# Moving the epilogue's transposes to another accumulator and the next head's block-maximum pass eight iterations later, in an eight-core attention kernel

## The chip, the cores and the metric

The kernel runs on all eight cores of one Trainium2 chip, four cores on each of two dies. Every core gets two of the sixteen sequences and runs the same program on them; nothing is exchanged between cores. The metric is the device time of the slowest core in microseconds (us): the median of three runs before is 6212.64 us (6209.49 to 6223.26).

## What is computed

The output is `x + attention(xn) + ffn(xn)`, with `xn` the layer norm of `x`, shape 16 x 2048 x 1024. The attention has 16 heads of 64 columns and selects 32 x 32 blocks:

```
Qh, Kh, Vh = block means of Q, K, V over 32 rows
low  = Qh @ Kh.T / 8 ; row_max = low.max(-1)
norm = low - row_max + 5000 near the diagonal
hi_mask = norm >= (1024th largest value of norm)
hi   = Q_block @ K_block.T / 8 for the selected blocks      # exact scores
max_vals = running maximum of hi per query
num  = sum exp(hi - max_vals) @ V, corrected, + low part for the other blocks
den  = the same sums without V, corrected, + 1e-6
out  = num / den
```

The running maximum enters the result in the kernel only through the small constant of the denominator, so each head needs, beside the sums of exponentials, a maximum of its scores over every selected 32 x 32 block.

## The kernel before

Engines are TensorE (PE), VectorE (DVE), ScalarE (ACT), GpSimd (POOL) and SyncE (SP, it only issues DMAs). A recorder writes one instruction list for each engine; each list runs in order. Every instruction except those of PE first waits for the one before it on its own engine, and every DMA of an SP or POOL list waits for the landing of the DMA before it in that list. All ordering between engines is by counting semaphores.

The program first normalises `x`, transposes the weights, runs the feed-forward half and the threshold search; it writes `x + ffn` to the DRAM array `part_sc`. The attention stage follows, from about 2300 us to the end. It has eight passes, one for each pair of heads. A pass does

1. the projections of Q and K for both heads (`qtp`, `ktp`), 128 matmuls into the two halves of the PSUM tile `pA`,
2. the V projection and its transposes, between which the block-maximum pass (called phase A here) of the first unit runs,
3. four units: two heads by two sequences. Unit 0 is the first one of a pass, unit 3 the last.

A unit is 32 iterations `kg` (`emit_chunk_iter`, L824). Iteration `kg` issues on PE two score matmuls S(kg) into `pS[kg % 2]` (L835), then two matmuls AV(kg-1) (L801) that add the product of the exponentials with V into `pO`, then, if there is a next unit in the pass, two halves of phase A for that next unit (`emit_phaseA_half`, L746): one matmul of 512 columns into one half of `pA` (L758), and on DVE a maximum over each group of 32 columns (L766); every fourth half adds the mask `bx` and reduces once more (L773, L776). ACT does one exponential of 128 x 1024 an iteration (L848). There are 64 halves to a unit, so two an iteration in units 0 to 2, and none in unit 3. After iterations 15 and 31 ACT copies `pO` to `outT` (L820, called the evacuation here).

`emit_prep` (L699) is called for the next unit before the 32 iterations. On POOL's list it waits for the end of the last unit's matmuls and then issues four DMAs, one after another: `rhsc`, `lhsc`, `bx`, `rmb` (L705 to L713). Half 0 of phase A waits on PE for the landing of `bx`. On SP's list it loads the slice of `part_sc` for the next unit into `xtile` (L719). On DVE it writes the mask rows of `rhsc` (L724) and three small tiles; ACT turns these into `laT` (L740).

The epilogue (`emit_epilogue`, L853) follows the unit: 16 transposes of `outT` with 128 columns each into `pS[0]` and `pS[1]` (L860), two additions and one reciprocal on DVE (L869, L874), 16 activations of 128 x 64 that scale into `stage` (L881), an addition of `xtile` on POOL (L891) and the store (L895). Since `pS` is used, S(0) of the next unit waits for all 16 activations:

```
if kg == 0:
    r.wait("tensor", "sGP", state["ngp_prep"][par])
    r.wait("tensor", "sDV", state["ndv_prep"][par])
    r.wait("tensor", "sDV", state["ndv_ep"])
    r.wait("tensor", "sAC", state.get("nac_ep", 0))
```

The addition stands in POOL's list ahead of the next `emit_prep`.

Of the kernel before, what the change touches and what calls it, by code (L numbers as in the profile page):

```python
# [11 lines left out]
AF = mybir.ActivationFunctionType  # L12
ALU = mybir.AluOpType
# [82 lines left out]
def build_program(debug=False, trunc=None):  # L96
# [17 lines left out]
    part_sc = nc.dram_tensor("part_sc", [T, C], F32).ap()  # L114
# [18 lines left out]
    with stack:  # L133
        r = Rec(nc, stack)
# [6 lines left out]
        id_f = sb("id_f", [128, 128], F32)  # L141
# [16 lines left out]
        eps_all = sb("eps_all", [128, NBH * 16], F32)  # L158
# [47 lines left out]
        with contextlib.ExitStack() as st_p0:  # L206
# [135 lines left out]
            def bh_idx(p, hip, s):  # L342
                return (2 * p + hip) * 2 + s
# [304 lines left out]
        with contextlib.ExitStack() as st_p2:  # L648
# [33 lines left out]
            def bh_idx(p, hip, s):  # L682
# [14 lines left out]
                     "nst_a2": [0, 0]}  # L697

            def emit_prep(p, hip, sq, par, prev_chunk_pe):  # L699
                b = bh_idx(p, hip, sq)  # L700
# [45 lines left out]
            def emit_phaseA_half(p, hip, sq, u):  # L746
# [105 lines left out]

            def emit_epilogue(p, hip, sq, par):  # L853
                b = bh_idx(p, hip, sq)
                r.wait("tensor", "sAC", state["prev_evac"])
                r.wait("tensor", "sDV", state["ndv_ep"])
                slot_off = [0, 128, 256, 384, 512, 640, 768, 896]
                for i in range(16):
                    so = slot_off[i % 8]
                    r.emit("tensor", lambda e, i=i, so=so: e.transpose(  # L860
                        pS[i // 8][:, so:so + 65],
                        outT[:, i * 128:(i + 1) * 128], id_f[0:65, 0:65]))
                npe_tr = r.cnt["sPE"]
                stg = stage2[par]
                r.wait("vector", "sPE", npe_tr)
                r.wait("vector", "sSY", state["nst_a2"][par])
                r.wait("scalar", "sSY", state["nst_a2"][par])
                for h2 in range(2):
                    r.emit("vector", lambda e, b=b, h2=h2: e.tensor_tensor(  # L869
                        rdenw16[:, h2 * 8:(h2 + 1) * 8],  # L870
                        pS[h2].ap().rearrange("p (a c) -> p a c", a=8)[:, :, 64:65]
                        .rearrange("p a c -> p (a c)"),
                        eps_all[:, b * 16 + h2 * 8:b * 16 + (h2 + 1) * 8], ALU.add))
                ndv_rd = r.emit("vector", lambda e: e.reciprocal(  # L874
                    rdenw16[:, :], rdenw16[:, :]))
                r.wait("scalar", "sDV", ndv_rd)
                nac_ep = 0
                for i in range(16):
                    so = slot_off[i % 8]
                    nac_ep = r.emit("scalar", lambda e, i=i, so=so, stg=stg:  # L880
                                    e.activation(  # L881
                                        stg[:, i * 64:(i + 1) * 64],
                                        pS[i // 8][:, so:so + 64], AF.Identity,
                                        scale=rdenw16[:, i:i + 1]))
                state["ndv_ep"] = r.cnt["sDV"]
                state["nac_ep"] = nac_ep
                h = 2 * p + hip
# [12 lines left out]
            state["nls_next"] = 0  # L900
            for p in range(8):
# [11 lines left out]
                for tag, dst in [("q", qtp), ("k", ktp)]:  # L913
                    for n in range(8):
                        slot = n % 2
                        r.wait("tensor", "sAC", pcons[slot])
                        r.wait("tensor", "sDV", state["phA_dv2"][slot])
# [22 lines left out]
                for half in range(2):  # L940
                    vev = [0] * 4
                    for n4 in range(4):
                        n = half * 4 + n4
                        slot = n % 2
                        r.wait("tensor", "sAC", pcons[slot])
                        r.wait("tensor", "sDV", state["phA_dv2"][slot])
# [48 lines left out]
                for i in range(4):  # L995
# [8 lines left out]
                    emit_epilogue(*bhs[i], par)  # L1004
# [80 lines left out]
```

How the kernel before makes its waits and increments, by code:

```python
    def emit(self, eng, fn):  # L57
        sname = ESEM[eng]
        n = 16 if eng in ("sync", "gpsimd") else 1
        if eng != "tensor" and self.cnt[sname]:
            self.wait(eng, sname, self.cnt[sname])
        self.cnt[sname] += n
        h = self.sem[sname]
        self._push(eng, lambda e, fn=fn, h=h, n=n: fn(e).then_inc(h, n))
        return self.cnt[sname]
# [1 line left out]
    def wait(self, eng, sname, val):  # L67
        if not val:
            return
        h = self.sem[sname]
        self._push(eng, lambda e, h=h, v=val: e.wait_ge(h, v))
```

## Time and profile before

| what | value |
|---|---|
| median of the runs | 6212.64 us |
| the profiled execution's own time | 6235.19 us |
| span of its slowest core (core 1) | 6233.6 us |
| spans of all cores | 6191.9 to 6233.6 us |
| PE / DVE / ACT / POOL busy | 50% / 40% / 27% / 3% of the span |
| DVE L766, 2048 reductions | 1416.7 us busy |
| ACT L848, 1024 exponentials | 1048.6 us busy |
| PE L758, L835, L801, 2048 each | 872.5, 696.4, 678.5 us busy |

The profiled execution is one of many, and 22.6 us longer than the median. "Busy" is a share of the whole span, which has stages with different limits. PEclk is the clock that TensorE was granted, as a share of 2.4 GHz: 1.00 is 2.4 GHz and 0.50 is 1.2 GHz.

### The profile page before, as it was taken

How to read it: one execution, taken by the hardware profiler on the slowest of the kernel's cores; microseconds unless marked ns; L12 is line 12 of the kernel's file. 1: busy time of each engine (PE TensorE's matmuls, PEld its weight loads, DVE VectorE, ACT ScalarE, POOL GpSimd, SP SyncE). 2: the span in 40 equal slices, each digit the busy share in tenths (PEclk: the TensorE clock that was granted, in tenths of full speed). 3: DMA queues.
4: the chain of work that ended last, by engine and by line, in shares of the span. 5: the costliest groups of instructions: out<-in, count | busy, mean ns of one | idle time of the engine just before them, and what ended most of it. 6: DMA issues, size and time to landing. Idle time of an engine off the chain costs nothing.

```text
span 6233.6 us, 53657 instructions; the slowest of 8 cores (6191.9 to 6233.6 us)
## 1 busy us (share of the span) xinstructions
PE 3145.2 (50%) x11513; PEld 1101.5 (18%) x11513; DVE 2502.1 (40%) x5239; ACT 1708.6 (27%) x2627; POOL 212.2 (3%) x269
## 2 busy tenths in 40 slices
PE   1121113333333426666666666566566666657656
PEld 0021001111111111122222112122122112112112
DVE  3522133343344315533633552551561551642553
ACT  2200000000000002452442343344344334335235
POOL 0000100000000000000000000000000000000000
PEclk9955557667766856776886777787687678678678
DMA  1243002222212310001001001000100010010010
GB/s 61 63 81 68 2 15 68 67 59 64 68 41 59 83 46 23 18 14 29 14 17 23 21 17 23 21 14 17 29 14 17 16 28 16 18 28 14 14 24 11
DMA packets 457371, 206.62 MB, mean 33 GB/s; under 512 B 428746, under 2 KB 429938, under 8 KB 456882
## 3 DMA queue, kind: packets, MB, share of 16 engines
q1 hardware_dynamic: 420946, 138.85, 9.1%
q0 software_dynamic: 36128, 64.34, 4.4%
q8 instruction: 121, 1.98, 0.1%
q14 instruction: 176, 1.44, 0.1%
HBM read 150.62 MB, written 47.73 MB: 32 GB/s over the span
## 4 chain that ended last, share of the span: by engine, by line
PE 30%; DMA 23%; DVE 22%; ACT 12%; issue 11%; DVEq 1%; ACTq 0%; POOL 0%; POOLq 0%; SPq 0%
DVE bm L766 10%; PE pA L758 7%; PE pS L835 6%; ACT aT L848 6%; PE pO L801 5%; DMA bx<-bsm_dram 4%; PE pA L920 4%; DMA fW<-wT_r 3%; ACT stage L881 3%; PE pA L516 3%; DMA fW<-wT_v 2%; DMA fW<-wT_k 2%; DMA rhsc<-qtp 2%; DMA nb<-norm_all 2%; DVE fA L501 2%
## 5 line engine op out<-in xcount | busy, mean ns | idle before, releaser
L766 DVE TENSOR_REDUCE bm<-pA 128x16 f32<-128x512 f32 x2048 | 1416.7, 692 | 1340.0 <-PE pA L758 1152.5
L848 ACT ACTIVATE aT<-pS 128x1024 bf16<-128x1024 f32 x1024 | 1048.6, 1024 | 1176.8 <-PE pS L835 1144.8
L758 PE MATMUL pA<-ktp,qtp 64*128 64x512 bf16 x2048 | 872.5, 453 | 805.6 <-DMA bx<-bsm_dram 477.9
L835 PE MATMUL pS<-rhsc,lhsc 128*128 128x512 bf16 x2048 | 696.4, 426 | 216.9 <-ACT stage L881 186.4
L801 PE MATMUL pO<-aT,vtm 128*65 128x512 bf16 x2048 | 678.5, 416 | 196.1 <-ACT aT L848 187.3
L516 PE MATMUL pA<-fA,fW 128*128 128x512 bf16 x1536 | 414.6, 422 | 291.8 <-DMA fW<-wT_r 75.7
L758 PEld LDWEIGHTS pA<-ktp,qtp 64*128 64x128 bf16 x2048 | 186.6, 96 | 1478.4 <-issue 1469.4
L417 PE MATMUL pB<-bis_cnt,ones 128*128 128x32 f32 x116 | 35.1, 396 | 684.4 <-DVE bis_cnt L413 684.4
L801 PEld LDWEIGHTS pO<-aT,vtm 128*65 128x65 bf16 x2048 | 223.0, 120 | 538.0 <-issue 458.1
L869 DVE TENSOR_TENSOR rdenw<-pS,eps_all 128x8 f32<-128x8 f32 x64 | 10.7, 167 | 616.9 <-PE pS L860 612.5
L516 PEld LDWEIGHTS pA<-fA,fW 128*128 128x128 bf16 x1536 | 151.2, 105 | 549.4 <-issue 438.5
L835 PEld LDWEIGHTS pS<-rhsc,lhsc 128*128 128x128 bf16 x2048 | 142.0, 101 | 546.7 <-issue 501.8
L547 ACT ACTIVATE fR<-pA 128x512 bf16<-128x512 f32 x64 | 38.2, 597 | 717.1 <-PE pA L516 717.1
L920 PE MATMUL pA<-xnT,wsl_q 128*128 128x512 bf16 x512 | 135.1, 434 | 169.3 <-DMA out<-stage 104.5
L881 ACT ACTIVATE stage<-pS,rdenw 128x64 f32<-128x64 f32 x512 | 160.8, 314 | 150.5 <-DVE rdenw L874 106.0
L581 ACT ACTIVATE fA<-fB 128x512 bf16<-128x512 bf16 x64 | 40.3, 629 | 477.4 <-DVE fB L574 472.3
L986 ACT ACTIVATE vtm<-pS 128x64 bf16<-128x64 f32 x256 | 57.5, 224 | 392.4 <-PE pS L977 390.2
L547 ACT ACT_TABLE_LOAD x1 | 1.3, 1283 | 596.4 <-PE pA L516 596.4
L891 POOL TENSOR_TENSOR stage<-stage,xtile 128x1024 f32<-128x1024 f32 x32 | 74.7, 2336 | 2401.4 <-ACT stage L881 2401.4
L417 PEld LDWEIGHTS pB<-bis_cnt,ones 128*128 128x128 f32 x116 | 29.0, 311 | 694.0 <-issue 694.0
L949 PE MATMUL pA<-xnT,wsl_v 128*128 128x512 bf16 x512 | 137.5, 436 | 2.2 <-DVE bm L766 2.2
L773 DVE TENSOR_TENSOR bmm<-bm,bx 128x64 f32<-128x64 f32 x512 | 115.5, 226 | 53.2
(139 smaller groups left out, 2307.9 us busy)
## 6 DMA issues: line engine op xcount, KB each, us to landing
xtile<-x SPq DMA_DIRECT2D x64, 512.0 KB
fW<-wT_r SPq DMA_DIRECT2D x64, 256.0 KB
fW<-wT_k SPq DMA_DIRECT2D x64, 256.0 KB
fW<-wT_v SPq DMA_DIRECT2D x64, 256.0 KB
xtile<-part_sc SPq DMA_DIRECT2D x32, 512.0 KB
bx<-bsm_dram POOLq DMA_DIRECT2D x32, 512.0 KB, 8.0
out<-stage SPq DMA_DIRECT2D x32, 512.0 KB
part_sc<-ptile POOLq DMA_DIRECT2D x16, 512.0 KB, 3.0
```

Of the source, the lines that this page charges most:

```text
L501: e.scalar_tensor_tensor(d[:, c * QT:(c + 1) * QT], xnT[:, base:base + QT], mucol[m][:, c:c + 1], d[:, c * QT:(c + 1) * QT], ALU.mult, ALU ...
L516: e.matmul(pA[:, sl * 512:sl * 512 + QT], w[:, cc * 128:(cc + 1) * 128], rb[:, cc * QT:(cc + 1) * QT], start=(cc == 0), stop=(cc == 7)))
L758: e.matmul(pA[:, half * 512:(half + 1) * 512], qtp[p0:p0 + 64, ts0 + t * 128:ts0 + (t + 1) * 128], ktp[p0:p0 + 64, ts0 + kq * 512:ts0 + (k ...
L766: nred = r.emit("vector", lambda e, kq=kq, half=half: e.tensor_reduce(bm[:, kq * 16:(kq + 1) * 16], pA[:, half * 512:(half + 1) * 512] .re ...
L773: r.emit("vector", lambda e, b=b, t=t: e.tensor_tensor(bmm[:, :], bm[:, :], bx[:, t * 64:(t + 1) * 64], ALU.add))
L801: e.matmul(pO[:, sl * 512:(sl + 1) * 512], vtm[:, (sq * 16 + k) * 130 + hip * 65: (sq * 16 + k) * 130 + hip * 65 + 65], aT[bpar][:, sl * 5 ...
L835: e.matmul(pS[bpar][:, sl * 512:(sl + 1) * 512], lhs2[par][:, k * 128:(k + 1) * 128], rhs2[par][:, qh * 1024 + sl * 512: qh * 1024 + (sl + ...
L848: e.activation(aT[bpar][:, :], pS[bpar][:, :], AF.Exp, scale=0.125))
L881: e.activation(stg[:, i * 64:(i + 1) * 64], pS[i // 8][:, so:so + 64], AF.Identity, scale=rdenw16[:, i:i + 1]))
L891: "gpsimdc", lambda e, par=par, stg=stg: e.tensor_tensor(stg[:, :], stg[:, :], xtile[par][:, :], ALU.add))
L920: e.matmul(pA[:, slot * 512:(slot + 1) * 512], wsl[tag][:, cc * 128:(cc + 1) * 128], xnT[:, cc * T + n * 512:cc * T + (n + 1) * 512], star ...
L949: e.matmul(pA[:, slot * 512:(slot + 1) * 512], wsl["v"][:, cc * 128:(cc + 1) * 128], xnT[:, cc * T + n * 512: cc * T + (n + 1) * 512], sta ...
```

## The change

Three things are done.

- The epilogue of units 0 to 2 no longer uses `pS`. Its 16 transposes go in two waves of eight into `pA`. Wave 0 (eight transposes, one addition, one reciprocal, eight activations) stands at the end of the unit; wave 1 stands in iteration 4 of the next unit, after AV(3) on PE and ahead of exponential 4 on ACT, and with it the POOL addition and the store. S(0) waits for neither. The epilogue of unit 3 stays as it was.
- Phase A of the next unit, which `pA` is needed for, is spread over iterations 8 to 31: three halves in each of iterations 8 to 23, two in each of iterations 24 to 31. Iterations 0 to 7 have none.
- The load of the `part_sc` slice is issued again just ahead of its use (in `finish`), while the load in `emit_prep` stays: 32 loads of 512 KB more.

```diff
@@ emit_phaseA_half
+                if u < 2:
+                    r.wait("tensor", "sAC", state["pA_free_ac"][half])
+                    r.wait("tensor", "sDV", state["ndv_ep"])
@@ emit_chunk_iter
                 if kg == 0:
                     r.wait("tensor", "sGP", state["ngp_prep"][par])
                     r.wait("tensor", "sDV", state["ndv_prep"][par])
-                    r.wait("tensor", "sDV", state["ndv_ep"])
-                    r.wait("tensor", "sAC", state.get("nac_ep", 0))
@@
-                if nxt is not None:
-                    emit_phaseA_half(*nxt, 2 * kg)
-                    emit_phaseA_half(*nxt, 2 * kg + 1)
+                if kg == 4 and state["pending_w1"] is not None:
+                    state["pending_w1"]()
+                    state["pending_w1"] = None
+                if nxt is not None and kg >= 8:
+                    if kg < 24:
+                        us = range((kg - 8) * 3, (kg - 8) * 3 + 3)
+                    else:
+                        us = range(48 + (kg - 24) * 2, 48 + (kg - 24) * 2 + 2)
+                    for u in us:
+                        emit_phaseA_half(*nxt, u)
@@ emit_epilogue, units 0 to 2 (unit 3 keeps the old form)
+                    r.wait("tensor", "sDV", max(state["phA_dv2"][0],
+                                                state["phA_dv2"][1]))
+                    def emit_wave(w, gate0=0, gate1=0):
+                        if gate0:
+                            r.wait("tensor", "sAC", gate0)
+                        acts = []
+                        for sl8 in range(8):
+                            i = w * 8 + sl8
+                            if gate1 and sl8 == 4:
+                                r.wait("tensor", "sAC", gate1)
+                            r.emit("tensor", lambda e, i=i, sl8=sl8: e.transpose(
+                                pA[:, sl8 * 128:sl8 * 128 + 65],
+                                outT[:, i * 128:(i + 1) * 128], id_f[0:65, 0:65]))
...
+                        ndv_rd = r.emit("vector", lambda e, w=w: e.reciprocal(
+                            rdenw16[:, w * 8:(w + 1) * 8],
+                            rdenw16[:, w * 8:(w + 1) * 8]))
+                        r.wait("scalar", "sDV", ndv_rd)
...
+                        for sl8 in range(8):
+                            i = w * 8 + sl8
+                            acts.append(r.emit(
+                                "scalar", lambda e, i=i, sl8=sl8, stg=stg:
+                                e.activation(stg[:, i * 64:(i + 1) * 64],
+                                             pA[:, sl8 * 128:sl8 * 128 + 64],
+                                             AF.Identity,
+                                             scale=rdenw16[:, i:i + 1])))
+                        return ndv_rd, acts
+                    _, acts0 = emit_wave(0)
+                    def w1fn(acts0=acts0, b=b, par=par, stg=stg, h=h, sq=sq):
+                        ndv_rd, acts1 = emit_wave(1, gate0=acts0[3], gate1=acts0[7])
+                        state["ndv_ep"] = ndv_rd
+                        state["nac_ep"] = acts1[7]
+                        state["pA_free_ac"] = [acts1[3], acts1[7]]
+                        finish(b, par, stg, h, sq, acts1[7])
+                    state["pending_w1"] = w1fn
@@ new function, the end of every epilogue
+            def finish(b, par, stg, h, sq, nac_ep):
+                r.wait("sync", "sGC", state["ngp_add"][par])
+                nld = r.emit("sync", lambda e, h=h, sq=sq, par=par: e.dma_start(
+                    xtile[par].ap().rearrange("p (i d) -> p i d", i=16),
+                    part_sc.rearrange("(s i pp) c -> s pp i c", i=16, pp=128)
+                    [sq][:, :, h * 64:(h + 1) * 64]))
                 r.wait("gpsimdc", "sAC", nac_ep)
-                r.wait("gpsimdc", "sSY", state["nsy_part"][par])
+                r.wait("gpsimdc", "sSY", nld)
```

The projections' waits on `pA` take the later of their old value and the waves' last activations.

## Rows read from the trace of the kernel before

**Rows 1.** Who waited for whom, core 1: us in total, times, longest us.
```profile
PE pA L758 <- DMA bx<-bsm_dram: 477.9, 32, 18.8
...
PE pS L835 <- ACT stage L881: 186.4, 24, 8.0
```

**Rows 2.** Timeline between units 0 and 1 of the third pass: start, us, engine, instruction.
```profile
3516.50 1.02 ACT L820 ACTIVATE outT<-pO 65x1024 f32<-65x1024 f32 x1 [2.32 <-PE pO L810]
...
3517.77 1.97 PE L860 MATMUL pS<-id_f,outT 65*128 65x65 f32 x16 [1.42 <-ACT outT L820]
3519.98 0.44 DVE L869 TENSOR_TENSOR rdenw<-pS,eps_all 128x8 f32<-128x8 f32 x2 [7.38 <-PE pS L860]
...
3520.92 6.41 ACT L881 ACTIVATE stage<-pS,rdenw 128x64 f32<-128x64 f32 x16 [3.40 <-DVE rdenw L874]
...
3527.43 0.35 ACT L740 ACTIVATE laT<-la_t,cln 64x64 bf16<-64x64 f32 x1
...
3528.64 1.02 ACT L848 ACTIVATE aT<-pS 128x1024 bf16<-128x1024 f32 x1 [0.87 <-PE pS L835]
3529.90 0.57 POOL L705 DMA_DIRECT2D rhsc<-qtp  x1
...
3546.80 1.01 PE L758 MATMUL pA<-ktp,qtp 64*128 64x512 bf16 x2 [18.30 <-DMA bx<-bsm_dram]
```

**Rows 3.** Windows from evacuation to the first reduction L766, 16 units 1 and 2: columns below.
```profile
core 1: us, PE busy (x) PEld busy (x) DVE busy (x) ACT busy (x) POOL busy (x), PEclk, DMA share, GB/s
...
3516.50:3547.55 31.05, 3.73 (x20) 2.15 (x20) 2.40 (x7) 7.42 (x19) 4.55 (x5) 0.50 0.30 68
...
sum 488.09, PE 59.74 PEld 34.30 DVE 38.45 ACT 118.64 POOL 72.88; mean PE 3.73 PEld 2.14 DVE 2.40 ACT 7.42 POOL 4.55
```

**Rows 4.** Windows from first to last reduction L766, 16 units 1 and 2; then sum of 8 units 0.
```profile
3547.55:3613.06 65.51, 55.90 (x189) 16.39 (x188) 50.97 (x94) 31.74 (x31) 0.26 (x1) 0.91 0.01 1
...
sum 1059.55, PE 897.06 PEld 263.22 DVE 815.25 ACT 507.86 POOL 4.08; mean PE 56.07 PEld 16.45 DVE 50.95 ACT 31.74 POOL 0.25
...
sum 535.38, PE 462.23 PEld 133.73 DVE 407.67 ACT 253.93 POOL 2.49; mean PE 57.78 PEld 16.72 DVE 50.96 ACT 31.74 POOL 0.31
```

**Rows 5.** Timeline of ACT in unit 1, third pass: exponentials 4 iterations apart, 2.4 GHz.
```profile
3557.20 1.02 ACT L848 ACTIVATE aT<-pS 128x1024 bf16<-128x1024 f32 x1 [0.48 <-PE pS L835]
...
3564.86 1.02 ACT L848 ACTIVATE aT<-pS 128x1024 bf16<-128x1024 f32 x1 [0.56 <-PE pS L835]
```

**Rows 6.** The chain that ended last, one iteration of unit 0 at 1.2 GHz.
```profile
3447.51 0.97 PE pS L835 x2
...
3449.33 0.97 PE pA L758 x2
3450.30 0.97 PE pS L835 x2
```

**Rows 7.** Timeline of ACT in unit 3 of the third pass: pairs of exponentials, no phase A.
```profile
3738.70 2.14 ACT L848 ACTIVATE aT<-pS 128x1024 bf16<-128x1024 f32 x2 [0.20 <-PE pS L835]
3741.05 2.14 ACT L848 ACTIVATE aT<-pS 128x1024 bf16<-128x1024 f32 x2 [0.20 <-PE pS L835]
```

**Rows 8.** Windows from exponential 0 to exponential 8, the 8 units 3.
```profile
3731.34:3742.16 10.82, 9.41 (x30) 2.96 (x28) 0.00 (x0) 8.19 (x8) 1.30 (x1) 0.77 0.24 50
...
sum 84.98, PE 72.43 PEld 22.89 DVE 0.00 ACT 65.54 POOL 10.41; mean PE 9.05 PEld 2.86 DVE 0.00 ACT 8.19 POOL 1.30
```

**Rows 9.** Windows from the V stage's last reduction to unit 0's first one, sum of 8.
```profile
sum 152.71, PE 14.13 PEld 2.72 DVE 20.90 ACT 17.04 POOL 17.46; mean PE 1.77 PEld 0.34 DVE 2.61 ACT 2.13 POOL 2.18
```

**Rows 10.** Windows: feed-forward half, V stage, and unit 1 around its middle evacuation.
```profile
1596.00:1604.00 8.00, 3.77 (x16) 1.42 (x16) 1.31 (x5) 1.19 (x2) 0.00 (x0) 1.00 0.15 35
3352.00:3380.00 28.00, 19.54 (x43) 4.29 (x42) 22.27 (x41) 6.33 (x28) 0.40 (x1) 0.50 0.02 1
...
3582.00:3589.30 7.30, 7.30 (x18) 1.69 (x19) 3.90 (x7) 2.89 (x3) 0.00 (x0) 0.55 0.00 0
```

**Rows 11.** Timeline of SP in unit 1, third pass: the load in `emit_prep`.
```profile
3534.99 0.36 SPq L719 DMA_DIRECT2D xtile<-part_sc  x1
```

More of the change, by code:

```diff
@@ L696, in build_program @@
                      "pcons": [0, 0], "nac_qk": 0, "nsy_part": [0, 0], "ngp_add": [0, 0],
-                     "nst_a2": [0, 0]}
+                     "nst_a2": [0, 0], "pA_free_ac": [0, 0], "pending_w1": None}
             def emit_prep(p, hip, sq, par, prev_chunk_pe):
@@ L851, in emit_chunk_iter, with emit_epilogue @@
                 state["prev_exp"][kpar] = newexp
-            def emit_epilogue(p, hip, sq, par):
+            def emit_epilogue(p, hip, sq, par, last):
                 b = bh_idx(p, hip, sq)
+                stg = stage2[par]
+                h = 2 * p + hip
                 r.wait("tensor", "sAC", state["prev_evac"])
[L856 to L887, printed above, removed]
@@ new lines, in emit_epilogue @@
+                if last:
+                    r.wait("tensor", "sAC", max(state["prev_exp"][0],
+                                                state["prev_exp"][1]))
+                    slot_off = [0, 128, 256, 384, 512, 640, 768, 896]
+                    for i in range(16):
+                        so = slot_off[i % 8]
+                        r.emit("tensor", lambda e, i=i, so=so: e.transpose(
+                            pS[i // 8][:, so:so + 65],
+                            outT[:, i * 128:(i + 1) * 128], id_f[0:65, 0:65]))
+                    npe_tr = r.cnt["sPE"]
+                    r.wait("vector", "sPE", npe_tr)
+                    r.wait("vector", "sAC", state["nac_ep"])
+                    for h2 in range(2):
+                        r.emit("vector", lambda e, b=b, h2=h2: e.tensor_tensor(
+                            rdenw16[:, h2 * 8:(h2 + 1) * 8],
+                            pS[h2].ap().rearrange("p (a c) -> p a c", a=8)
+                            [:, :, 64:65].rearrange("p a c -> p (a c)"),
+                            eps_all[:, b * 16 + h2 * 8:b * 16 + (h2 + 1) * 8],
+                            ALU.add))
+                    ndv_rd = r.emit("vector", lambda e: e.reciprocal(
+                        rdenw16[:, :], rdenw16[:, :]))
+                    r.wait("scalar", "sDV", ndv_rd)
+                    r.wait("scalar", "sSY", state["nst_a2"][par])
+                    nac_ep = 0
+                    for i in range(16):
+                        so = slot_off[i % 8]
+                        nac_ep = r.emit("scalar", lambda e, i=i, so=so, stg=stg:
+                                        e.activation(
+                                            stg[:, i * 64:(i + 1) * 64],
+                                            pS[i // 8][:, so:so + 64], AF.Identity,
+                                            scale=rdenw16[:, i:i + 1]))
+                    state["ndv_ep"] = ndv_rd
+                    state["nac_ep"] = nac_ep
+                else:
+                    r.wait("tensor", "sDV", max(state["phA_dv2"][0],
[10 more added lines that the diff above has]
+                                pA[:, sl8 * 128:sl8 * 128 + 65],
+                                outT[:, i * 128:(i + 1) * 128], id_f[0:65, 0:65]))
+                        npe_tr = r.cnt["sPE"]
+                        r.wait("vector", "sPE", npe_tr)
+                        if w == 0:
+                            r.wait("vector", "sAC", state["nac_ep"])
+                        r.emit("vector", lambda e, b=b, w=w: e.tensor_tensor(
+                            rdenw16[:, w * 8:(w + 1) * 8],
+                            pA.ap().rearrange("p (a c) -> p a c", a=8)
+                            [:, :, 64:65].rearrange("p a c -> p (a c)"),
+                            eps_all[:, b * 16 + w * 8:b * 16 + (w + 1) * 8],
+                            ALU.add))
+                        ndv_rd = r.emit("vector", lambda e, w=w: e.reciprocal(
+                            rdenw16[:, w * 8:(w + 1) * 8],
+                            rdenw16[:, w * 8:(w + 1) * 8]))
+                        r.wait("scalar", "sDV", ndv_rd)
+                        if w == 0:
+                            r.wait("scalar", "sSY", state["nst_a2"][par])
+                        for sl8 in range(8):
[9 more added lines that the diff above has]
+                    def w1fn(acts0=acts0, b=b, par=par, stg=stg, h=h, sq=sq):
+                        ndv_rd, acts1 = emit_wave(1, gate0=acts0[3],
+                                                  gate1=acts0[7])
+                        state["ndv_ep"] = ndv_rd
+                        state["nac_ep"] = acts1[7]
+                        state["pA_free_ac"] = [acts1[3], acts1[7]]
+                        finish(b, par, stg, h, sq, acts1[7])
+                    state["pending_w1"] = w1fn
+                    return
@@ L888, in emit_epilogue @@
+                finish(b, par, stg, h, sq, state["nac_ep"])
+            def finish(b, par, stg, h, sq, nac_ep):
[4 more added lines that the diff above has]
+                    [sq][:, :, h * 64:(h + 1) * 64]))
                 r.wait("gpsimdc", "sAC", nac_ep)
-                r.wait("gpsimdc", "sSY", state["nsy_part"][par])
+                r.wait("gpsimdc", "sSY", nld)
@@ L915, in build_program @@
                         slot = n % 2
-                        r.wait("tensor", "sAC", pcons[slot])
-                        r.wait("tensor", "sDV", state["phA_dv2"][slot])
+                        r.wait("tensor", "sAC",
+                               max(pcons[slot], state["pA_free_ac"][slot]))
+                        r.wait("tensor", "sDV",
+                               max(state["phA_dv2"][slot], state["ndv_ep"]))
                         for cc in range(8):
@@ L944, in build_program @@
                         slot = n % 2
-                        r.wait("tensor", "sAC", pcons[slot])
-                        r.wait("tensor", "sDV", state["phA_dv2"][slot])
+                        r.wait("tensor", "sAC",
+                               max(pcons[slot], state["pA_free_ac"][slot]))
+                        r.wait("tensor", "sDV",
+                               max(state["phA_dv2"][slot], state["ndv_ep"]))
                         for cc in range(8):
@@ L1003, in build_program @@
                     state["chunk_pe_end"] = r.cnt["sPE"]
-                    emit_epilogue(*bhs[i], par)
+                    emit_epilogue(*bhs[i], par, i == 3)
                 if debug and p == 0:
```

## The prediction

> **What bounds the kernel now.** I read the page first, then the waits, then the stretches between units in time order, and last windows laid over the same stretch in all eight passes. The page has no engine above 50% of the span, so no single engine bounds the kernel; each stage must be taken alone. The change touches only the four units of each pass, and there the list of waits names two stalls of PE: 477.9 us for `bx` in 32 waits, and 186.4 us for the epilogue's activations in 24 waits, 7.8 us each [rows 1]. The reader should look at the timeline for how they lie. After the evacuation at 3516.50 come the transposes, two additions, a reciprocal and 16 activations; exponential 0 starts at 3528.64, 12.1 us after the evacuation. Then the first POOL DMA goes out only at 3529.90, behind the addition, and half 0 of phase A, which waits for the third DMA, starts at 3546.80, with everything else of the unit queued behind it on PE [rows 2]. Over the 16 units 1 and 2 the way from evacuation to the first reduction takes 488.09 / 16 = 30.5 us, with PE busy for 3.7 us of it [rows 3].
>
> Behind that start the unit is bound by DVE. With the clock at 2.4 GHz four iterations take 3564.86 - 3557.20 = 7.66 us, 1.92 us each, or 0.958 us for each half of phase A, and 64 halves take 61.3 us [rows 5]. Measured from first to last reduction it is 1059.55 / 16 = 66.2 us in units 1 and 2 and 535.38 / 8 = 66.9 us in units 0 [rows 4]. The rest, 4.9 and 5.6 us, is the cold start and the pause at the middle evacuation: at 1.2 GHz an iteration takes 3450.30 - 3447.51 = 2.79 us with PE busy throughout [rows 6], 0.87 us more than warm. Unit 3 has no phase A; there two exponentials take 2.35 us, so ACT bounds it at 1.17 us an iteration [rows 7].
>
> So phase A is work of DVE that the change keeps in full. What it can win is the time before phase A starts, and what it can lose is iterations 0 to 7 that were hidden under phase A before.
>
> **Part by part.** *Exponential 0.* Wave 0 has eight transposes where there were 16: 1.97 / 2 = 1.0 us. They start 1.27 us after the evacuation's start, as now. From the transposes' end to the first activation it is now 3520.92 - 3519.74 = 1.18 us; with one addition fewer (0.44 / 2 and the gap behind it) about 0.9. Eight activations take half of 6.41, 3.2 us, and `laT` holds exponential 0 for another 0.4 (its start to the next one's earliest) [rows 2]. Sum 1.27 + 1.0 + 0.9 + 3.2 + 0.4 = 6.8 us in place of 12.1. S(0) and S(1) are done by then.
>
> *Wave 1.* In iteration 4 it stands between exponentials 3 and 4. AV(3) waits for exponential 3 (1.03 us), takes 0.5 to 1.0 us, the transposes 0.5 to 1.0 (half of 1.97 at 1.2 GHz, half of that again at 2.4), DVE 0.9, the activations 3.2: 6.1 to 7.1 us from one exponential to the next where 1.17 is normal. I take 6.75, so 5.6 us more. What was removed in front (5.3 us) comes back here in full: S(0)'s freedom by itself is worth nothing. PE is queued behind too, AV(4) waits for exponential 4, so PE idles for some 4 us.
>
> *Iterations 0 to 7 without phase A.* Units 3 show what eight of them cost from a cold PE: 84.98 / 8 = 10.6 us [rows 8]. The idle time in wave 1 lets the clock fall again. Unit 1 shows this at its middle evacuation: the 7.3 us behind the pause have a clock of 0.55 [rows 10]. A cold start costs 10.6 - 8 x 1.17 = 1.3 us, and I charge it a second time. Exponential 8 is then at 6.8 + 10.6 + 5.6 + 1.3 = 24.3 us after the evacuation. Half 0 follows behind AV(7), the reduction about 1.2 us after exponential 8: 25.5 us, where it is 30.5 now. Gain 5.0 us in each of 16 units. If PE were cold through all eight iterations (4 matmuls, 1.93 us each, from the 0.97 us of two [rows 6]) it would be 28 and the gain 2.5.
>
> The `bx` landing doesn't hold this. The add leaves its place ahead of `emit_prep` in POOL's list, so the three DMAs start at the evacuation instead of 13.4 us later, and they need the 15 to 17 us that they need now [rows 2]: `bx` is there at about 17 us, covered by iterations 0 to 7. If that cover were gone the first reduction would be at 17 us, not later than now.
>
> *Unit 0* has no wave 1 in front of it. The way from the V stage's last reduction to its first one is 152.71 / 8 = 19.1 us [rows 9], and the `bx` chain sets it: with POOL's list unchanged there, it stays 19.1. The eight iterations fit in just before. Gain 0 here.
>
> *Phase A, three halves an iteration.* DVE needs 3 x 0.958 = 2.87 us for three halves; ACT needs 1.17 and PE seven matmuls of 0.22 us at 2.4 GHz. The two halves of `pA` suffice for it: four other matmuls come between, 0.86 us, less than the two reductions that are then still to run. So 61.3 us stays the floor. Of the 4.9 us above it I take away the cold start of two iterations, 1.7 us, since PE has run four full iterations before phase A begins, and leave the middle pause: 64.6 us. Gain 1.6 in units 1 and 2, and 66.9 - 64.6 = 2.3 in units 0. Best case 62.5, worst about 67.
>
> *Unit 3* has wave 1 of unit 2, but no phase A to win. Evacuation to exponential 8 is now 12.1 + 10.6 = 22.7 us and becomes 24.3: a loss of 1.6, call it 1.5 to 2. The tail after the last reduction and the last epilogue are as before.
>
> *The second load.* SP's list waits for no late event of PE there; both loads go out right behind the last store. Before, the load went out at 3534.99, 5 us behind the store ahead of it [rows 11], so a load costs about that, and wave 1 comes some 70 us later. In unit 3 the load has 30 us of cover. Price nothing; without the cover 5 us in each pass, 40 us.
>
> *Sum.* A pass: 2 x (5.0 + 1.6) + 2.3 - 1.6 = 13.9 us; eight passes 111 us. Against the profiled execution's 6235.2 us this gives 6124; its distance of 22.6 us to the median is kept, so the median is 6212.6 - 111 = 6101 us. Say 6102.
>
> **What the clock could do.** Windows of the feed-forward half show 1.00 with eight matmuls in 4 us [rows 10]. The new stretch has seven in 2.87 us, more than that, so once warm it should stay warm. The V stage shows the other side: at 0.50 it stays, with PE busy 19.5 of 28 us [rows 10]. Entered cold, three halves an iteration keep PE busy longer than that, 3.3 of at most 3.8 us, so it should warm up as in unit 1 now. The Trainium skill, page "TensorE: Matmul & The Clock Gate", section "A second HAM failure mode: psum-queue depth-cycling", speaks against it: PE micro-idles between groups of matmuls often enough that the clock oscillates, and throughput is lost between bursts. By that page the longer stretches in which PE waits for reductions of the new stretch would cost clock; by the rows they would not.
>
> **The rivals.** *A, cold stretch (slower).* If iterations 8 to 23 run at 1.2 GHz, a third half in an iteration adds its matmul and the wait for the first half's reduction, about 1.05 us, to 2.79: 3.83 in place of 2.87, 15.4 us a unit, 24 units, 369 us: 6470. For it speaks the V stage, against it the feed-forward rows. It decides the sign from 111 / 24 / 0.96, about 5 of the 16 iterations cold. That is the mechanism of the skill's section as it would act here.
>
> *B, the gaps of wave 1 cost more.* PE cold through iterations 0 to 7, the first reduction at 28 us, and no gain inside phase A: 2 x 2.5 - 3 = 2 us a pass, about 6195. For it speaks that PE is idle for some 4 us twice in a short time; against it that eight iterations in unit 3 take only 10.6 us after an idle time of 8 us.
>
> *C, more is won.* Phase A from first to last reduction at 62.5 us in all 24 units adds 2.1 x 24 = 50 us: 6051. For it: the middle pause gets three halves of cover in place of two.
>
> *D, no change.* The epilogue was only moved and DVE sets the time: iterations 0 to 7 eat the whole gain. This needs the first reduction at 30 us, which the working above gives only with a second stall.
>
> **How the numbers follow.** Forecast, 6060 to 6150: 0.62. Weaker with B between it and 6195: 0.16. C below 6060: 0.08. A: 0.09. D: 0.05. The range 6052 to 6190 leaves out A, D and little of B and C. A measurement of this kernel tells 0.2%, 12 us, from no change. Faster 0.84, same 0.06, slower 0.10.
>
> **What would show it.** Right: evacuation to exponential 0 near 6.8 us; exponential 3 to 4 near 6.8; evacuation to first reduction near 25.5 in units 1 and 2 and 19 in units 0, with the wait for `bx` gone except there; three halves in 2.87 us at a clock of 1.00; unit 3 longer by 1.6. Wrong: a PEclk of 0.50 over iterations 8 to 23, iterations 3.8 us long; or POOL's DMAs of `emit_prep` not starting at the evacuation.

## The result

The changed kernel takes 6459.03 us (median of 8 runs) beside 6222.63 us for the kernel before in the same rounds: a ratio of 1.038, 95% interval 1.037 to 1.040. It is slower by 236 us, where 111 us less were forecast. The profiled execution has a span of 6460.4 us on its slowest core, with a mean clock of 0.678 where it was 0.731 before. In some executions of any kernel here one die shows a clock lower by about 0.01 and takes up to 1% longer, so some numbers below are taken from cores 0 to 3, which show no such dip in the profiles compared.

The waits of the kernel after, core 3 (in total, times, longest), answer to [rows 1]:

```profile
PE pA L761 <- DVE bm L769: 400.1, 687, 1.5
...
PE pA L761 <- DMA bx<-bsm_dram: 111.2, 16, 13.4
```

The wait for `bx` fell from 477.9 to 111.2 us, and what is left of it belongs to the V stages and to units 0. The wait for the epilogue's activations (186.4 us before) is no longer in the list. Both stalls that the change aims at went, and yet the kernel is slower. A wait of PE for DVE came in their place, 687 times and never longer than 1.5 us; before, it was 333 times and 142.4 us in all. The kernel that repeats the scores (below) has just as much of this wait and not the loss, so the wait by itself is not the cause.

Windows over the same stretches as before tell where the time is. The sums are, in order: evacuation to first reduction in the 16 units 1 and 2 (answers to [rows 3]), one such unit from first to last reduction and the sum of 16, the sum of the 8 units 0 (both [rows 4]), and unit 3 from evacuation to evacuation, sum of 8.

```profile
sum 413.73, PE 241.65 PEld 96.31 DVE 40.85 ACT 249.43 POOL 77.56; mean PE 15.10 PEld 6.02 DVE 2.55 ACT 15.59 POOL 4.85
...
4227.73:4305.93 78.20, 63.27 (x157) 14.97 (x156) 50.94 (x94) 23.52 (x23) 0.00 (x0) 0.63 0.03 7
...
sum 1252.02, PE 1010.64 PEld 239.45 DVE 815.21 ACT 376.49 POOL 0.00; mean PE 63.16 PEld 14.97 DVE 50.95 ACT 23.53 POOL 0.00
...
sum 654.88, PE 545.27 PEld 126.10 DVE 407.59 ACT 188.21 POOL 3.70; mean PE 68.16 PEld 15.76 DVE 50.95 ACT 23.53 POOL 0.46
...
sum 457.20, PE 327.37 PEld 114.19 DVE 5.91 ACT 318.37 POOL 18.74; mean PE 40.92 PEld 14.27 DVE 0.74 ACT 39.80 POOL 2.34
```

The reader should see that DVE does exactly the same work in the units as before (50.95 us each), while the stretch that holds it grew from 66.2 to 1252.02 / 16 = 78.3 us in units 1 and 2 and from 66.9 to 654.88 / 8 = 81.9 us in units 0, and that the clock there is 0.63 where it was 0.91. All growth is in phase A: 2 x 12.0 + 15.0 = 39.0 us a pass. The first reduction comes 4.6 us earlier, twice a pass, and unit 3 is 1.4 us longer. Together that is 31.2 us a pass and 250 us; V stages and the starts of passes are some 20 us shorter in this profile, and the span grew by 226.8 us (6233.6 to 6460.4).

The clock can be watched as it falls. In unit 1 of the third pass phase A begins at 3603 with the clock at 1.00 ("warm"; 0.50 is "cold"), and six microseconds later, at 3609, it falls (the columns are those of [rows 3]):

```profile
3604.00:3608.00 4.00, 3.18 (x12) 0.95 (x11) 2.99 (x6) 1.26 (x2) 0.00 (x0) 1.00 0.49 107
3608.00:3612.00 4.00, 3.07 (x8) 0.78 (x7) 3.21 (x6) 1.35 (x2) 0.00 (x0) 0.65 0.44 94
...
3644.00:3648.00 4.00, 3.31 (x8) 0.72 (x7) 2.54 (x4) 1.02 (x1) 0.00 (x0) 0.50 0.00 0
```

It then stays at 0.50 for 58 us, until the iterations with two halves have begun. One such cold iteration in the timeline:

```profile
3644.42 1.02 ACT L856 ACTIVATE aT<-pS 128x1024 bf16<-128x1024 f32 x1 [3.04 <-PE pS L836]
...
3645.06 1.03 PE L761 MATMUL pA<-ktp,qtp 64*128 64x512 bf16 x2
...
3646.78 0.58 PE L761 MATMUL pA<-ktp,qtp 64*128 64x512 bf16 x1 [0.69 <-DVE bm L769]
...
3647.29 1.04 PE L836 MATMUL pS<-rhsc,lhsc 128*128 128x512 bf16 x2
...
3648.48 1.02 ACT L856 ACTIVATE aT<-pS 128x1024 bf16<-128x1024 f32 x1 [3.04 <-PE pS L836]
```

From exponential to exponential it takes 4.06 us. Two phase A matmuls go, PE waits 0.69 us for a half of `pA`, the third goes, and only then the next scores; ACT idles for 3.04 us. This is the iteration of rival A, priced at 3.83 us. Over iterations 16 to 23 of all 24 units the mean is 3.78 us, since the first of them follows the middle evacuation and is short.

### The profile page after: what moved, and what is told of

It is laid out like the page before. It is cut to its first block, busy times and chain, and to the rows that moved or that the text cites. A ratio compares the mean times of both kernels' runs of the same rounds, so it can differ in the third digit from the quotient of the medians.

```text
span 6460.4 us, 53953 instructions; the slowest of 8 cores (6428.6 to 6460.4 us)
## 1 busy us (share of the span) xinstructions
PE 3586.7 (56%) x11513; PEld 1154.9 (18%) x11513; DVE 2505.4 (39%) x5263; ACT 1706.8 (26%) x2627; POOL 212.9 (3%) x269
## 4 chain that ended last, share of the span: by engine, by line
PE 36%; DVE 23%; DMA 19%; issue 11%; ACT 9%; DVEq 1%; ACTq 0%; POOL 0%; SPq 0%; POOLq 0%
DVE bm L769 11%; PE pO L804 9%; PE pA L761 8%; PE pS L836 8%; PE pA L995 4%; ACT aT L856 3%; DMA fW<-wT_r 3%; PE pA L516 2%; DMA fW<-wT_k 2%; DMA bx<-bsm_dram 2%; DMA fW<-wT_v 2%; ACT stage L934 2%; DMA nb<-norm_all 2%; DVE fA L501 2%; DVEq L71 1%
## 5 line engine op out<-in xcount | busy, mean ns | idle before, releaser
L761 PE MATMUL pA<-ktp,qtp 64*128 64x512 bf16 x2048 | 1029.8, 544 | 593.5 <-DVE bm L769 400.1
L804 PE MATMUL pO<-aT,vtm 128*65 128x512 bf16 x2048 | 863.4, 515 | 377.0 <-ACT aT L856 367.4
L836 PE MATMUL pS<-rhsc,lhsc 128*128 128x512 bf16 x2048 | 863.0, 519 | 29.0 <-DVE rhsc L724 29.0
L804 PEld LDWEIGHTS pO<-aT,vtm 128*65 128x65 bf16 x2048 | 266.0, 144 | 856.2 <-issue 824.9
L836 PEld LDWEIGHTS pS<-rhsc,lhsc 128*128 128x128 bf16 x2048 | 180.1, 113 | 411.5 <-issue 362.4
L1063 ACT ACTIVATE vtm<-pS 128x64 bf16<-128x64 f32 x256 | 57.2, 223 | 396.9 <-PE pS L1054 394.7
L934 ACT ACTIVATE stage<-pA,rdenw 128x64 f32<-128x64 f32 x384 | 120.5, 314 | 138.0 <-DVE rdenw L924 106.8
L779 DVE TENSOR_REDUCE mv_all<-bmm 128x1 f32<-128x64 f32 x512 | 112.7, 220 | 54.7 <-DVE bmm L776 2.8
```

The lines of the kernel that those rows point to most:

```text
L761: e.matmul(pA[:, half * 512:(half + 1) * 512], qtp[p0:p0 + 64, ts0 + t * 128:ts0 + (t + 1) * 128], ktp[p0:p0 + 64, ts0 + kq * 512:ts0 + (k ...
L779: e.tensor_reduce(mv_all[:, b * 16 + t:b * 16 + t + 1], bmm[:, :], axis=AX.X, op=ALU.max))
L804: e.matmul(pO[:, sl * 512:(sl + 1) * 512], vtm[:, (sq * 16 + k) * 130 + hip * 65: (sq * 16 + k) * 130 + hip * 65 + 65], aT[bpar][:, sl * 5 ...
L836: e.matmul(pS[bpar][:, sl * 512:(sl + 1) * 512], lhs2[par][:, k * 128:(k + 1) * 128], rhs2[par][:, qh * 1024 + sl * 512: qh * 1024 + (sl + ...
L934: e.activation(stg[:, i * 64:(i + 1) * 64], pA[:, sl8 * 128:sl8 * 128 + 64], AF.Identity, scale=rdenw16[:, i:i + 1])))
```

## The experiments

Theory 1: three halves an iteration leave PE too little to do at 2.4 GHz, the clock falls, and at 1.2 GHz PE and its wait for `pA` set the iteration. Theory 2: the waves in `pA`, or the second load, are at fault. Theory 3: three halves wait for the two halves of `pA` at any clock. All ratios are to the kernel before in the same rounds. Differences between two changed versions are between medians, often of different rounds; the kernel before moved by 12 us between them (6210.5 to 6222.6), so less than that says nothing.

### The two parts of the change alone

First the new spread of phase A in the kernel before, with nothing else changed:

```diff
-                if nxt is not None:
-                    emit_phaseA_half(*nxt, 2 * kg)
-                    emit_phaseA_half(*nxt, 2 * kg + 1)
+                if nxt is not None and kg >= 8:
+                    if kg < 24:
+                        us = range((kg - 8) * 3, (kg - 8) * 3 + 3)
+                    else:
+                        us = range(48 + (kg - 24) * 2, 48 + (kg - 24) * 2 + 2)
+                    for u in us:
+                        emit_phaseA_half(*nxt, u)
```

> Only the new spread of phase A (none in iterations 0 to 7, three halves in 8 to 23, two in 24 to 31); the epilogue stays in pS at the unit's end, with no second load. Theory 1 (the spread lets TensorE's clock fall, and the cold iterations are the whole loss): from first to last reduction 82 us in unit 0 and 78 in units 1 and 2 as in the changed kernel, PEclk near 0.5 there; the way from evacuation to the first reduction stays 30.5, since the bx chain still starts behind the addition; about 8 x (15 + 12 + 12) = 312 us over before, 6530 us. Theory 2 (the waves in pA or the second load cause it): phase A stays at 66 us and the time within 20 us of before, 6220 us.

Measured: 6569.82 us, ratio 1.057 (1.055 to 1.059). Evacuation to first reduction stayed at 30.5 us, phase A took 82.0 us in units 1 and 2 and 81.5 in units 0. The spread alone carries the whole loss, and more. It came out 40 us above the number given. In this profile the clock is 0.50 at the first reduction of all 16 units 1 and 2, behind a wait for `bx` (in the changed kernel it is 1.00 there), and they now take as long as units 0.

Then the other part: both waves at the unit's end in `pA`, the second load, the addition behind the next unit's loads on POOL, and two halves an iteration from iteration 0.

```diff
-                if kg == 4 and state["pending_w1"] is not None:
-                    state["pending_w1"]()
...
                     if i < 3:
                         emit_prep(*bhs[i + 1], (i + 1) % 2, state["chunk_pe_end"])
+                    if state["pending_w1"] is not None:
+                        state["pending_w1"]()
+                        state["pending_w1"] = None
```

> Only the other half: the epilogue of units 0 to 2 in two waves in pA, both at the unit's end, with the second load and with the POOL addition behind the next unit's four loads; phase A two halves an iteration from iteration 0. Theory 1: phase A stays warm, 66 us from first to last reduction; the bx chain starts at the evacuation, so evacuation to first reduction falls from 30.5 to about 18 us in 16 units; unit 3 as before; 200 us less, about 6015 us. Theory 2: phase A needs 78 us or more here too, and the time is above before, about 6300 us.

Measured: 5993.17 us, ratio 0.965 (0.963 to 0.966). Theory 2 falls: with waves and load in place phase A stays at 66.2 us and 224 us are won. Wave 1 in iteration 4 was not run by itself: both waves stand at the unit's end here.

### Is it the waves, or the place of the addition?

The kernel before with one thing changed, the order on POOL's list:

```diff
@@ emit_prep, behind the four DMAs on POOL
+                if state["pending_add"] is not None:
+                    state["pending_add"]()
+                    state["pending_add"] = None
@@ emit_epilogue
+                if (hip, sq) in ((0, 0), (0, 1)):
+                    state["pending_add"] = add_and_store
+                else:
+                    add_and_store()
```

> The kernel before, with one change: in POOL's list the four loads of emit_prep stand ahead of the addition of the unit before (units 1 and 2); epilogue in pS, two halves an iteration, one load of part_sc. If the bx chain alone made the wait at the unit's start, the first load goes out at the evacuation, evacuation to first reduction falls from 30.5 to 17 or 18 us in 16 units, phase A stays at 66 us: 200 us less, about 6015 us. If the epilogue's activations share the blame, the first reduction is no earlier than about 25 us: 6130 us.

Measured: 5996.95 us, ratio 0.965 (0.963 to 0.966), the same as with the waves. Evacuation to first reduction, sum of 16:

```profile
sum 276.20, PE 59.77 PEld 34.35 DVE 38.45 ACT 118.66 POOL 36.44; mean PE 3.74 PEld 2.15 DVE 2.40 ACT 7.42 POOL 2.28
```

That is 17.3 us where [rows 3] have 30.5. The waves, which were the larger part of the code, are worth nothing when both stand at the unit's end; the 2.3 us addition that stood ahead of four loads, and waited for the epilogue, was the stall.

### More work, less time

The changed kernel with the scores of iterations 8 to 23 computed twice into the same place:

```diff
+                if nxt is not None and 8 <= kg < 24:
+                    for sl in range(2):
+                        r.emit("tensor", lambda e, ...: e.matmul(
+                            pS[bpar][:, sl * 512:(sl + 1) * 512], ...,
+                            start=True, stop=True))
```

> The changed kernel with the two score matmuls of iterations 8 to 23 of units 0 to 2 issued twice (the same values again, 2 x 16 x 24 = 768 matmuls of 512 columns more). Theory 1: more work keeps the clock at 2.4 GHz; an iteration with three halves takes 2.87 us in place of 4.06, phase A 65 us, and the time falls to about 6110 us although work was added. Rival (three halves wait for the two halves of pA at any clock): PEclk may rise but the iteration stays near 4 us, and the time is 6460 us or, cold with 0.85 us more in each of 384 iterations, up to 6790 us.

Measured: 6164.09 us, ratio 0.992 (0.989 to 0.995). There are 768 matmuls more, and 295 us less than in the changed kernel. One unit 1 or 2, the sum of 16, and the sum of the 8 units 0, first to last reduction; then PE's wait for the reductions:

```profile
4087.68:4153.97 66.29, 49.78 (x187) 15.71 (x186) 50.95 (x94) 23.80 (x24) 0.00 (x0) 1.00 0.04 8
...
sum 1064.15, PE 796.94 PEld 253.10 DVE 815.27 ACT 379.69 POOL 0.00; mean PE 49.81 PEld 15.82 DVE 50.95 ACT 23.73 POOL 0.00
...
sum 553.61, PE 424.89 PEld 131.38 DVE 407.65 ACT 188.41 POOL 3.38; mean PE 53.11 PEld 16.42 DVE 50.96 ACT 23.55 POOL 0.42
...
PE pA L761 <- DVE bm L769: 402.1, 666, 1.5
```

The clock is 1.00 in all units 1 and 2 and 0.90 to 1.00 in units 0, phase A takes 66.5 and 69.2 us, and iterations 16 to 23 take 23.7 us where the changed kernel needs 30.2 (past the short first one, 3.2 us each in place of 4.06). PE is busy for less time (49.8 us) with 30 matmuls more than the changed kernel needs (63.2 us). That settles theory 1 against theory 3: the loss comes with the clock, and with the clock up the two halves of `pA` don't cost it. PE waits for the reductions as often and as long as in the changed kernel (402.1 and 400.1 us), so these short waits stand at either clock and don't decide it.

The same count of extra matmuls, but of phase A's own kind (64 rows of the array in place of 128):

```diff
-                r.emit("tensor", lambda e, ...: e.matmul(pA[:, half * 512:...], ...))
+                for _ in range(1 + extra):
+                    r.emit("tensor", lambda e, ...: e.matmul(pA[:, half * 512:...], ...))
...
+                        emit_phaseA_half(*nxt, u, int(kg < 24 and u % 3 != 2))
```

> The changed kernel with two of the three phase A matmuls of iterations 8 to 23 issued twice: the same count of 512-column matmuls more as the run that repeats the scores, but of the 64-row kind. If any matmul keeps the clock up, the iteration is 3.0 us and the time that of the repeated scores, about 6165 us. If what counts is also how much of the array a matmul uses (the scores use 128 rows and 128 columns, phase A 64 rows), the clock stays at 1.2 GHz or swings, iterations stay at 4 us or more and the time is 6460 us or above, up to 6790.

Measured: 6348.44 us, ratio 1.021 (1.020 to 1.023): between the two. It isn't a mean, though. The windows of two units 0:

```profile
2443.34:2508.05 64.71, 50.62 (x188) 14.76 (x186) 50.94 (x94) 23.55 (x23) 0.25 (x1) 1.00 0.01 1
...
3936.15:4024.15 88.00, 81.30 (x188) 20.20 (x186) 50.93 (x94) 23.56 (x23) 0.71 (x1) 0.57 0.01 1
```

The same instructions take 64.7 us or 88.0 us. Of the 24 units 11 lie between 64.6 and 66.8 us, seven of eight units 0 near 88, the rest between. The clock at the first reduction goes with it in units 0: 1.00 in the one of 64.7 us, 0.50 to 0.54 in the seven others. In the cold one shown PE is recorded busy for 81.3 of 88 us, and the clock comes back only after 76 us, when the iterations with two halves have begun. Here neither a busy PE in the records nor the count of matmuls told whether the clock would rise; the 128-row scores kept it at 1.00 in units 1 and 2 and brought it back soon in units 0, as many 64-row matmuls did not.

### The order of twos and threes

```diff
-                    if kg < 24:
-                        us = range((kg - 8) * 3, (kg - 8) * 3 + 3)
-                    else:
-                        us = range(48 + (kg - 24) * 2, 48 + (kg - 24) * 2 + 2)
+                    us = range((kg - 8) * 64 // 24, (kg - 7) * 64 // 24)
```

> The changed kernel with the same 64 halves over the same iterations 8 to 31, but in the order 2, 3, 3 throughout in place of 16 iterations with three and then 8 with two. The DVE work is the same. If an iteration with two halves between those with three is enough to bring the clock back, phase A takes 65 to 70 us and the time is 6110 to 6250 us. If the clock stays down through such a mix, all 24 iterations are cold at about 3.6 us: phase A 88 us, 8 x (6 + 10 + 10) = 208 us over the changed kernel, about 6670 us.

Measured: 6290.08 us, ratio 1.012 (1.010 to 1.014), neither of the two. Phase A takes 75.8 us in units 0 and 70.3 in the others; three of 24 units take 61.2 to 62.4, the floor of [rows 5], at a clock of 0.97 to 1.00. The fastest and the slowest of units 1 and 2:

```profile
3057.64:3118.85 61.21, 44.63 (x157) 13.36 (x156) 50.95 (x94) 23.55 (x23) 0.00 (x0) 1.00 0.08 18
...
5626.86:5706.28 79.42, 64.65 (x157) 15.21 (x156) 50.95 (x94) 23.55 (x23) 0.00 (x0) 0.63 0.03 7
```

These are the matmuls of the changed kernel with none added, so iterations with three halves can run at 1.00 and reach DVE's floor. That the clock makes the loss is so confirmed without extra work, and the kind and number of matmuls don't settle the clock alone. What makes it fall, the first part of theory 1, is not shown. With the same work in the same iterations 169 us are won by the order, and it still loses to the kernel before.

### The second load

The changed kernel without the load in `emit_prep`:

> The changed kernel without the first of the two loads of the part_sc slice. If the loads are hidden, as forecast, the time is that of the changed kernel within 13 us, 6459 us. If they cost what the trace shows for one on the path, 5 us a pass, 40 us less: 6420 us.

Measured: 6462.98 us, ratio 1.040 (1.038 to 1.042). 16.8 MB of loads more cost nothing, as forecast.

### Versions that beat both

In the kernel with the loads ahead of the addition, `bx` is loaded first and waits for the last phase A alone:

```diff
-                r.wait("gpsimd", "sPE", prev_chunk_pe)
                 r.wait("gpsimd", "sDV", state["phA_done_dv"])
...
-                state["ngp_bx"] = r.emit("gpsimd", lambda e, b=b: e.dma_start(bx[:, :], ...))
+                state["ngp_bx"] = r.emit("gpsimd", lambda e, b=b: e.dma_start(bx[:, :], ...))
+                r.wait("gpsimd", "sAC", after_ac)
+                r.wait("gpsimd", "sPE", prev_chunk_pe)
```

> The kernel with the loads ahead of the addition, and the load of bx ahead of the three others, waiting only for the end of the last phase A and for no matmul or projection. If the bx chain is what still delays the first reduction, evacuation to first reduction falls from 17.3 to about 13 us in units 1 and 2 (then the epilogue's activations set it), V stage to unit 0 from 19.1 to 12, and the wait at the start of the V stage (14 us) goes: about 237 us less, 5760 us. If something else is late next (rhsc and lhsc for S(0) of the unit after, the DMA queue), less than 60 us.

Measured: 5828.46 us, ratio 0.938 (0.936 to 0.939). Evacuation to first reduction is 12.7 us and V stage to unit 0 12.3 us, as expected, but only 169 us of 237 came. The start of a pass gained less than the 14 us expected: from the last evacuation of a pass to the V stage's first reduction it is 60.8 us where it was 64.8 (cores 0 to 3). The chain that ended last shows why; the store that ends a pass in this kernel, and in the one without `bx` first:

```profile
3633.20 10.34 DMA out<-stage
```
```profile
3677.58 3.81 DMA out<-stage
```

The `bx` load now runs beside that store, and the next pass waits for the store: 148.0 us in seven waits, where it was 104.5. So one wait more:

```diff
+                r.wait("gpsimd", "sSY", r.cnt["sSY"])
                 emit_prep(*bhs[0], 0, 0, r.cnt["sAC"])
```

> The kernel with bx loaded first, and one wait more: at the start of a pass POOL's list waits for the last unit's store before it loads bx. In the run with bx first the wait of the projections for that store rose from 104.5 to 148.0 us over 7 passes, since store and bx load run together. If that collision is the reason why the start of the V stage gained nothing, 44 us or somewhat more come back: 5828 - 44 = 5784 us, range 5775 to 5800. If bx is then late for the V stage instead, no change: 5828 us.

Measured: 5809.62 us, ratio 0.934 (0.931 to 0.937); its runs spread from 5779 to 5821. In the profile the projections' wait for the store is back at 105.1 us, and on cores 0 to 3 the way from the last evacuation of a pass to the V stage's first reduction is 54.7 us in place of 60.8. That is 6.1 us in each of seven passes, 43 us, the 44 expected; the median span of these four cores is 5772.0 us in this profile and 5810.0 in the one before, 38 less. The collision and its size are shown by the profiles; the medians of the runs show only 19 us of it.

Eight halves of phase A ahead of S(0), while ACT does the epilogue, then two in iterations 0 to 23 and one in 24 to 31:

```diff
                 if kg == 0:
+                    if nxt is not None:
+                        for u in range(8):
+                            emit_phaseA_half(*nxt, u)
```

> The kernel with bx loaded first, and eight halves of the next unit's phase A issued on PE ahead of S(0), while ACT does the epilogue; then two halves in iterations 0 to 23 and one in 24 to 31. If DVE's idle time at the unit's start is now what is left to win, the first reduction comes 7 us after the evacuation in place of 12.7, iterations 24 to 31 are bound by ACT at 1.17 us, and units 1 and 2 are 7 us shorter: 5828 - 16 x 7 = about 5720 us. If fewer matmuls in iterations 24 to 31, or the eight thin ones in front, keep the clock at 1.2 GHz, iterations take up to 2.3 and 2.8 us and the time is 5830 us or more.

Measured: 5817.62 us, ratio 0.936 (0.935 to 0.938), not told apart from the 5828 us without it. The first reduction did come at 6.8 us, but S(0) stands behind the eight halves and exponential 0 moved from 12.2 to 14.3 us, and iterations 24 to 29 take 1.38 us, not 1.17. Units 1 and 2 are 1.5 and 2.5 us shorter, not 7. With the wait for the store added:

> The same wait added to the kernel with eight halves of phase A in the gap. That one was at 5818 us, not told apart from 5828; its units 1 and 2 are 1.5 to 2.5 us shorter, 8 x 4 = 32 us, its units 0 one us longer, 8 us. With the collision gone about 5784 - 24 = 5760 us; if the halves in the gap are worth nothing, the same as the other kernel of this call.

Measured: 5770.43 us, ratio 0.928 (0.925 to 0.931). This is the fastest version, 7% below the kernel before. How much of the 39 us to the last but one is due to the eight halves stays open: the slowest cores of the two profiles lie 6 us apart (5777.0 and 5770.9).

## Why the prediction was wrong

The terms of the sum, in us, with what the windows of the changed kernel give:

| term | forecast | measured |
|---|---|---|
| evacuation to exponential 0, units 1 and 2 | 6.8 | 7.0 |
| exponential 3 to 4 with wave 1 | 6.75 | 6.4 |
| evacuation to first reduction, units 1 and 2 | 25.5 | 25.9 |
| V stage to first reduction, unit 0 | 19.1 | 19.2 |
| unit 3 | 57.3 | 57.2 |
| second load | 0 | 0 |
| phase A, units 1 and 2 | 64.6 | 78.3 |
| phase A, units 0 | 64.6 | 81.9 |

**What held.** Each term outside phase A is within half a microsecond: wave 0, wave 1 (which gives back what the freed S(0) wins), the second cold start, the `bx` chain hidden but in unit 0, and the loads at nothing. The prediction said that S(0)'s freedom is worth nothing by itself; the two runs at 5993 and 5997 us agree. B, C and D needed a first reduction at 28 us, a phase A of 62.5 us or a first reduction at 30 us; none came.

**The step that failed.** It is the sentence that the new stretch has seven matmuls in 2.87 us, more than the eight in 4 us at a clock of 1.00 in the feed-forward rows [rows 10], so that once warm it should stay warm. In its place the clock fell to 0.50 some six microseconds into phase A and an iteration with three halves took 4.06 us; phase A, put at 64.6 us, took 78.3 and 81.9. The difference is 2 x (78.3 - 64.6) + (81.9 - 64.6) = 44.7 us a pass, 357 us in all, which is the whole distance from 6102 to 6459; that it fits to the microsecond is luck, since smaller misses cancel (6 us more on the way to the first reductions, some 20 us less in V stages and starts of passes, 10 us more in the kernel before between the rounds). The comparison counted matmuls. The eight of the feed-forward half use 128 rows and 128 columns; of the seven here three use 64 rows and two write 65 columns. The run with repeated 64-row matmuls against the one with repeated scores shows that equal number is not enough, 6348 against 6164 us. That the kind of matmul is the reason is argued, not shown: the two kernels also differ in where in the iteration the extra matmuls stand. And there was a nearer witness for the same mixture: the iteration of the kernel before at 2.4 GHz has six matmuls in 1.92 us [rows 5], 12.5 in 4 us, beside which the new stretch, with 9.8, is the thinner one. The prediction did not compare with it. Why the clock falls in one unit and not in another stays open. Where it stayed up the rest of the term was near: 66.5 and 69.2 us with the scores repeated, 61.2 to 62.4 in three units of the even spread.

**The entry.** The second half of that step, that a stretch entered cold warms up because PE is busy in it, failed too. The V stage stood in [rows 10] with PE busy 19.5 of 28 us at 0.50. In a cold iteration of phase A PE is busy for 3.3 of 4 us, and the clock stays at 0.50 as well, until iterations with two halves come, in the first of which PE is busy throughout (4.00 of 4 us).

**The rivals.** A was the right mechanism with the right place and nearly the right price: 15.4 us a unit given over the forecast 64.6; measured over the same 64.6 it is 17.3 in units 0 and 13.7 in units 1 and 2, which start warm, 14.9 in the mean. Its time was 6470 us, measured 6459. It got a chance of 0.09. The Trainium skill, page "TensorE: Matmul & The Clock Gate", section "A second HAM failure mode: psum-queue depth-cycling", says that with micro-idles between groups of matmuls the clock oscillates. The trace agrees in part: with 687 waits of at most 1.5 us the clock fell, but it then stayed at 0.50 for 58 us, and with 666 such waits in the kernel that repeats the scores it was 1.00. The prediction overruled the page with a row that wasn't like the case. The abstract rule of that page, in section "HAM oscillation — how this bites in real kernels", looks for long idle gaps of PE only; here the clock fell in iterations whose longest one was 0.9 us.

**What the gain was.** The forecast asked what each wait costs, and not which of the two aims was worth it. One move on POOL's list, which the change makes by the way, wins 220 us (6217 to 5997) without any new spread of phase A.

## What to carry to other kernels

Before matmuls are gathered into fewer, DVE-bound iterations, look for a stretch of the same mixture of matmuls in the trace, not of the same number: here a stretch of full matmuls (128 rows, 128 columns) was a poor witness for one in which five of seven were thinner. When a loop is bound by another engine and PE's clock matters, adding work to PE is a cheap test: if the time falls and the clock in the rows rises, it was the clock. And read the in-order list of the engine that issues a late load before building anything else: an instruction that waits ahead of it is often the whole stall, and moving a load earlier needs a look at which store it will then run beside.

## What was not expected of the hardware

- The same stretch of instructions has two durations, 64.7 and 88.0 us, with clocks of 1.00 and 0.57, and which one it takes varies from unit to unit of one execution. In the even spread, with no matmul added, it is 61.2 and 79.4 us.
- 768 matmuls of 512 columns more made the kernel 295 us faster (6459 to 6164 us).
- PE was recorded busy for 81.3 of 88.0 us with the clock at 0.57, and for 44.6 of 61.2 us with the clock at 1.00: recorded busy time did not tell the clock.
- A store of 512 KB took 10.3 us beside one load of 512 KB from DRAM and 3.8 us without it.
